# A graph-transformer layer on one core: the query row of the edge loop goes through PSUM, copied there by ScalarE

## The reference, cut to what matters

```python
def _L0_gnn_ref(feats, edge_index, edge_attr, Wq, bq, Wk, bk, Wv, bv, Wo, bo):
    q, k, v = ...                       # feats @ W.T + b, as 8 heads of 32
    r, c = edge_index[:, 0], edge_index[:, 1]
    sim = jnp.einsum('hed,hed->eh', q[:, c, :], k[:, r, :]) * scale
    m = jax.ops.segment_max(sim, c, num_segments=bs)
    p = jnp.exp(sim - m[c])
    attn = p / jax.ops.segment_sum(p, c, num_segments=bs)[c]
    agg = jax.ops.segment_sum((attn.T[..., None] * v[:, r, :]).transpose(1, 0, 2)..., c, ...)
    return agg @ Wo.T + bo

xn = _layernorm(x)
x = x + _L0_gnn_ref(xn, [src, dst], ...) + _L0_mix_ref(xn, w_qkv, w_out, b_out)   # linear attention
x = x + _L0_ffn_ref(_layernorm(x), ...)      # 8 experts, one per token, capacity limited
```

## Time and profile before

| | |
|---|---|
| time, median of 3 runs | 3486.49 us (3481.72 to 3488.05) |
| the profiled execution's own time | 3486.49 us |
| its span, first to last instruction | 3485.3 us |
| VectorE busy | 2388.3 us, 69% |
| GpSimd busy | 2430.6 us, 70% |
| TensorE busy | 2314.7 us, 66% |
| ScalarE busy | 1002.9 us, 29% |

### The profile page before, as it was taken

One profiled execution on the slowest core, in us unless ns is written; L12 is line 12 of the kernel. 1 busy time (PEld: TensorE's weight loads), 2 busy tenths in 40 slices (PEclk: granted clock), 3 DMA queues, 4 the chain that ended last, 5 costly groups with the idle time before them and its releaser, 6 DMA issues. The chain is left out here.

```text
span 3485.3 us, 39176 instructions
## 1 busy us (share of the span) xinstructions
PE 2314.7 (66%) x9498; PEld 1804.6 (52%) x9499; DVE 2388.3 (69%) x3245; ACT 1002.9 (29%) x4232; POOL 2430.6 (70%) x2220
## 2 busy tenths in 40 slices
PE   2839337675676666676688768556555562659998
PEld 1527226554555555454466545444444442559998
DVE  2324249786776787698888867877888884636665
ACT  1513116454455455451011100000000000435543
POOL 5050578777777777787777777777777776447776
PEclk7858668887888788787888877776777876569999
DMA  4624466666666666667777777666666662823341
GB/s 132 207 71 146 123 174 177 187 189 189 185 178 183 187 184 180 188 190 200 217 219 218 221 210 214 189 179 179 182 188 181 185 182 99 286 75 86 81 95 25
DMA packets 258264, 590.77 MB, mean 170 GB/s; under 512 B 49410, under 2 KB 135505, under 8 KB 257565
## 3 DMA queue, kind: packets, MB, share of 16 engines
q0 software_dynamic: 150480, 467.10, 49.3%
q1 hardware_dynamic: 97947, 109.47, 9.5%
q10 hardware_dynamic: 9296, 9.44, 0.8%
HBM read 519.05 MB, written 71.76 MB: 170 GB/s over the span
## 5 line engine op out<-in xcount | busy, mean ns | idle before, releaser
L959 POOL DMA_INDIRECT wide<-kv_d,arena x1099 | 1262.7, 1149 | 368.8 <-issue 344.9
L1253 PE MATMUL ps<-wide,arena 128*128 128x264 f32 x2432 | 782.2, 482 | 373.8 <-issue 219.1
L1253 PEld LDWEIGHTS ps<-wide,arena 128*128 128x128 f32 x2432 | 573.1, 241 | 568.2 <-issue 275.0
L959 POOL DMA_INDIRECT arena<-kv_d,arena x539 | 623.6, 1157 | 182.8 <-issue 165.4
L1356 DVE TENSOR_REDUCE arena<-arena 128x64 f32<-128x2048 f32 x229 | 523.5, 2286 | 7.9
L1253 PE MATMUL ps<-arena 128*128 128x264 f32 x1216 | 385.4, 476 | 174.6 <-issue 103.6
L1353 DVE TENSOR_TENSOR arena<-wide 128x2048 f32<-128x2048 f32 x153 | 350.8, 2293 | 185.1 <-DMA wide<-kv_d,arena 173.8
L1253 PEld LDWEIGHTS ps<-arena 128*128 128x128 f32 x1216 | 283.0, 238 | 272.9 <-issue 135.1
L1389 DVE TENSOR_TENSOR wide<-wide,ps 128x2112 f32<-128x2112 f32 x152 | 356.8, 2347 | 77.8 <-issue 39.0
L134 PE MATMUL ps<-halves 128*128 128x256 f32 (+2 forms) x2304 | 361.3, 319 | 3.2 <-DVE halves L1622 1.6
L134 PEld LDWEIGHTS ps<-halves 128*128 128x128 f32 x2304 | 331.0, 192 | 30.9 <-POOL halves L1632 3.5
(11 more groups left out here) (319 smaller groups left out, 3343.1 us busy)
## 6 DMA issues: line engine op xcount, KB each, us to landing
wide<-kv_d,arena POOLq DMA_INDIRECT x1099
arena<-in_w SPq DMA_DIRECT2D x16, 1024.0 KB
kv_d<-wide SPq DMA_DIRECT2D x49, 260.0 KB
arena<-xn_d SPq DMA_DIRECT2D x98, 128.0 KB
arena<-kv_d,arena POOLq DMA_INDIRECT x539
hb_d<-arena SPq DMA_DIRECT2D x16, 516.0 KB, 4.4
q_d<-wide SPq DMA_DIRECT2D x49, 128.0 KB
xn_d<-arena SPq DMA_DIRECT2D x7, 896.0 KB, 8.0
```

Source lines behind the costliest of these rows:

```text
L959: e.indirect_dma_start(out=kvb[k][:, j, :], out_offset=None, in_=kv_d, in_offset=bass.IndirectOffsetOnAxis(ap=ixb[k][:, j:j + 1], axis=0)) ...
L1253: m = e.matmul(psE[(k + 1) % 3][:, 0:264], ident, kvb[b][:, j, 256:ROW], start=(j == 0), stop=(j == J - 1))
```

## The change

ScalarE copies the query row of the next step from SBUF into a PSUM bank that the loop did not use (`ps[2]`), right behind `e_prod` and ahead of its copy of the indices. VectorE's L1353 reads the row from there and waits for the new semaphore `e_q` as well. The offset of the row is now loaded by ScalarE and no longer by VectorE.

```diff
-        p_ps, S_ps = ps[3][:, 0:8 * J], S_sb
+        q_ps, p_ps, S_ps = ps[2][:, 0:256], ps[3][:, 0:8 * J], S_sb
...
         def _(e):                                   # scalar
             e.wait_ge(e_n0, 1)
+            e.activation(q_ps, qsf[:, 0:256], ACT.Copy).then_inc(e_q, 1)
...
-                e.load([w_], tabF[:, bass.ds(at * 4 + 2, 1)])
+                e.load([w_, q_at], tabF[:, bass.ds(at * 4 + 2, 2)])
                 e.load([t6, w6, p6], tabF[:, bass.ds(at * 4 + 4 * RING - 1, 3)])
                 e.wait_ge(e_prod, g_)
+                e.activation(q_ps, qsf[:, bass.ds(val(e, q_at, NT * BLK) * 5, 256)], ACT.Copy).then_inc(e_q, 1)
                 e.activation(ixb[k], ixf[...], ACT.Copy).then_inc(e_ix, 1)
...
-            def scores(k, count, arrived, q_row):
+            def scores(k, count, arrived):
+                e.wait_ge(e_q, count)
                 e.wait_ge(e_arr[k], arrived)
                 e.tensor_tensor(prod.rearrange("p (j n) -> p j n", n=256), kvb[k][:, :, 0:256],
-                                q_row.unsqueeze(1).to_broadcast([128, J, 256]), ALU.mult).then_inc(e_prod, 1)
+                                q_ps.unsqueeze(1).to_broadcast([128, J, 256]), ALU.mult).then_inc(e_prod, 1)
...
-                e.load([ar, p, w_, q_at], tabF[:, bass.ds(val(e, cg, CH - 14) * 4, 4)])
+                e.load([ar, p, w_], tabF[:, bass.ds(val(e, cg, CH - 14) * 4, 3)])
...
-                scores((k + 1) % RING, cn, ar, qsf[:, bass.ds(val(e, q_at, NT * BLK) * 5, 256)])
+                scores((k + 1) % RING, cn, ar)
```

## The result

The changed kernel took 3511.61 us (median of four runs, 3503.78 to 3516.84) where the kernel before took 3484.10 beside it (3478.4 to 3488.05): a ratio of 1.0079, with an interval of 1.0056 to 1.0101. Forecast were 3367 us. The sign is wrong, and the mechanism at the centre of the forecast, gathers held by the product's second SBUF operand, is right.

What follows compares the result with a forecast made beforehand. GpSimd was taken to bound the edge loop, with VectorE 214 us behind. The span's 3485.3 − 214.0 + 70 + 25 = 3366.3, plus 1.2 around it, gave 3367 us; range for 8 in 10: 3285 to 3432.

Steps and rivals of the forecast that it cites:

- The gathers are held by a second SBUF operand: GpSimd's gathers beside VectorE's L1353, which reads two SBUF tensors, are held up; 325 us in all.
- GpSimd at 2120 us: GpSimd's edge loop once gathers are free: 2438 − 325 + about 7 for small operations.
- without a pause: GpSimd was said to work through the whole edge loop: 1886.3 us busy plus 551.6 idle ahead of gathers.
- The hidden copy: ScalarE's query copy and address, 0.48 us a step, 109 us in all, fit its idle time; no cost in ordinary steps.
- the bound of −10: VectorE's product reading PSUM: its own time changes by 0, between −10 and +20 ns each, ±5 us.
- VectorE's other waits stay: VectorE's waits other than for gathers remain, such as L1389's 155.8 us for ScalarE and short ones at L1370.
- floor of 2243: VectorE's loop of about 2457 us needs about 2243 without its 214.0 us of gather waits, and sets the end.
- The new wait, 14 × 5.0 = 70 us: VectorE's product waits for a late ScalarE copy, 5.0 us more in each of 14 steps; bounds 0 and 85.
- 25 us not won: Gather waits of VectorE ahead of long ScalarE waits, 14 × 1.8 us, give no gain; bounds 0 and 40.
- A: Rival: VectorE's new wait costs nothing because ScalarE's lateness moves with VectorE; 3273 us, chance 0.12.
- B: Rival: where base tiles move beside gathers, DMA transfers take 64 us of the gain; 3431 us, chance 0.13.
- C: Rival: gathers are still held beside the product, GpSimd stays the bound, the new wait is paid; 3541 us, chance 0.06.

Runs made afterwards that it cites:

- first comparison: The changed kernel against the kernel before, on a chip that is not known: 3511.61 us against 3484.10, ratio 1.0079.
- half the sums: TensorE adds only every second edge's values; in the changed kernel 3060.41 us (0.9123) on chip 4, 3497.50 us (1.0033) on chip 3.
- GpSimd paused: The "one copy" kernel with six chained small memsets on GpSimd ahead of every step's gathers, on chip 4: 3658.92 us, 1.0907 of the kernel before.
- the wait alone: The changed kernel with copy and wait, but the product reads SBUF as before; against the kernel before 1.0063 on chip 9, 0.9979 on chip 14.
- one copy again: The "one copy" kernel repeated on chip 14, against the kernel before: 3063.01 us, 0.9123.
- one copy: The changed kernel with the query row copied to PSUM once ahead of the loop and no per-step wait, on chip 9: 3531.15 us, 1.0053 of before.

## Why the prediction was wrong

The chips seen are of two kinds, and what the change does hangs on the kind (profiled executions; idle time is VectorE's, in the loop):

| | before, us | change, ratio | before: loop, idle | change: loop, idle | held-up matmuls, full sums |
|---|---|---|---|---|---|
| chips 2, 4, 14 | 3354 to 3357 | 0.9126 | 2397, 464 | 2120, 204 | none |
| first comparison, chips 3, 9 | 3484 to 3511 | 1.0079, 1.0073 | 2461, 528 | 2522, 599 | 175 to 333 us |

The loops are those of chip 2 (before) and chip 14 (change), and of the first comparison. The unaltered change ran on one chip of the first kind; on chip 4 it ran with half the sums and came out the same. On the second kind it ran in the first comparison and on chip 3, not on chip 9. No chip is known to have been measured at two different times, so "kind of chip" can also mean what else the machine was doing then. On the second kind VectorE's idle time stays between 516 and 614 us in all nine profiles: with the wait or without, with freed gathers or held ones, with half the sums. On the first kind it follows the gathers: 452 to 464 us with held ones, 202 to 204 with free ones, 766 with GpSimd paused. I take the cause of the difference to be in the machine, not in the program: the same program shows it on some chips and not on others. What it is stays open. That instructions reach the engines late is one candidate, since single ones come in steps of 0.7 and 1.4 us. The queue that loads them moves as much (502 packets, 4.11 MB, 0.4% of the DMA engines' time) in either, which does not tell how late they come; TensorE's mean granted clock is 0.80 after in the first comparison and 0.84 on chip 14, which at that size explains no spacing of 2.8 us. No run tried another placement of instructions.

By the prediction's own steps:

**The gathers are held by a second SBUF operand: right,** on both kinds. Gathers of the change on chip 14, and of before on chip 2 (min/median/max ns):

```profile
L959 POOL DMA_INDIRECT wide<-kv_d,arena x1099: 947/953/1214, 386.5 to 2470.3; - x184
```
```profile
L959 POOL DMA_INDIRECT wide<-kv_d,arena x1099: 949/953/3066, 389.8 to 2763.1; - x184
```

By the Trainium skill's page "SBUF — State Buffer", section "Who interferes with whom", a VectorE instruction with two inputs in SBUF contends with a GpSimd instruction that reads SBUF; the traces agree, and "the wait alone", with its 1162 ns, bears it out again. The same section's inference that a tensor_tensor does not hold back the making of DMA descriptors does not hold for these gathers: up to 3.07 us beside one, at most 1.21 with the operand in PSUM.

**GpSimd at 2120 us: near, and by luck closer than it looks.** VectorE's loop on chip 14 is 2120.1 us. But what the prediction summed, the gathers and the idle time ahead of them, is 2085 us there, and its starting value of 2438 held hold-ups: the idle part is 551.6 us in the first comparison and 499.2 on chip 2, so "without a pause" was wrong by some 50 us. Page groups on chip 14:

```profile
L959 POOL DMA_INDIRECT wide<-kv_d,arena x1099 | 1054.1, 959 | 344.2 <-issue 332.5
L959 POOL DMA_INDIRECT arena<-kv_d,arena x539 | 517.8, 961 | 169.1 <-issue 163.7
...
L1106 ACT ACTIVATE ps<-arena 128x64 f32<-128x64 f32 x228 | 51.9, 228 | 1004.0 <-DVE arena L1410 995.9
...
L1356 DVE TENSOR_TENSOR arena<-wide,ps 128x2048 f32<-128x2048 f32 x153 | 349.0, 2281 | 48.2 <-DMA wide<-kv_d,arena 48.1
L1392 DVE TENSOR_TENSOR wide<-wide,ps 128x2112 f32<-128x2112 f32 x152 | 356.6, 2346 | 0.0
...
L1373 DVE TENSOR_TENSOR arena<-arena,ps 128x264 f32<-128x264 f32 x230 | 96.7, 420 | 95.0 <-issue 94.8
```

GpSimd is busy 1571.9 us and idle 513.3, of which 496.1 are the gap between two gathers. VectorE is close behind: of its 2120 us it is busy in some 1917 and idle in 204, of which 95 are at the turn, 27 at the ends of tiles and 55 for gathers. The hidden copy holds too ("one copy again" is within 0.2 us). The product's time fell by 11 ns, 2.5 us in all, a little beyond the bound of −10; the 65 ns of the prediction's estimate for a PSUM source do not appear. Both kinds agree in this.

**"VectorE's other waits stay": the step that failed.** The sum took away the 214 us of waits for gathers and kept VectorE's floor of 2243, with 70 + 25 us for the new wait. In the first comparison the waits for gathers went as forecast, to 10 us, but the rest of VectorE's idle time, 528 − 214 = 314 us, did not stay: it became 599 − 10 = 589. That is 275 us more where 95 were in the sum. With 28 us that came back behind the loop it made the profiled execution 36 us longer, where 119 less were forecast.

The premise behind it was that these waits belong to the program. I took L1389's 155.8 us for ScalarE's own lateness. On the first kind of chip they are 0.5 us in the kernel before, and VectorE waits 330 us for gathers in place of 214:

```profile
L1389 DVE TENSOR_TENSOR wide<-wide,ps 128x2112 f32<-128x2112 f32 x152 | 356.7, 2347 | 0.5 <-ACT arena L1105 0.5
L1353 DVE TENSOR_TENSOR arena<-wide 128x2048 f32<-128x2048 f32 x153 | 351.4, 2297 | 272.1 <-DMA wide<-kv_d,arena 271.3
```

The floor there is 2397 − 330 = 2067 us and not 2243, GpSimd's 2085 stand above it, and the change wins 291 us, 172 more than forecast (119); 277 of them are in the loop. The forecast is as wrong on this kind as on the other, only with the right sign.

**The new wait, 14 × 5.0 = 70 us, and 25 us not won.** That the idle time not for gathers is 595 us (614 − 19) in "one copy" as well shows that the wait is not what makes it grow. On chip 14 the product waits for ScalarE's copy 5.7 us in all. Why hold-ups fill whatever the gathers give back on the second kind is not explained by any run; it is only measured. On chip 9 the held-up spacing is 212 us with held gathers ("the wait alone") and 272 to 333 in the three kernels with free ones, so it grows with the pace of the gathers but is not made by it alone. The 25 us had a slip of their own: 1.8 us is the mean of those waits that are not zero, and over all 14 steps it is 1.4, so 20 us.

**The rivals.** A's mechanism, that the new wait costs nothing, holds on chip 14, but its time of 3273 is 0.939 of the kernel before and not 0.9126, since it keeps the same floor. B (transfers take part of the gain) is refuted there: where base tiles move (1300 to 1600 us) the DMA engines are busy 0.82 of the time at 244 GB/s, and in the whole loop VectorE waits 55 us for gathers in place of 330. C gave the right sign on the second kind for a wrong reason: no gather is held. None of the rivals had the machine itself in it, though the trace spoke of it. In the list of waits of the kernel before, from the first comparison:

```profile
ACT ps L1104 <- issue: 575.9, 136, 9.2
...
POOL wide L959 <- issue: 344.9, 1079, 8.4
```

and on chip 2:

```profile
ACT ps L1104 <- DVE arena L1407: 1205.9, 227, 9.4
...
POOL wide L959 <- issue: 333.4, 1094, 0.3
```

(Engine, tile, line, what was waited for: us in all, times, longest.) ScalarE, which on chip 2 waits for VectorE 227 times of 228, waited 576 us for nothing that the profile shows, and GpSimd's gap of 0.3 us once lasted 8.4. I put the first down as spare time of ScalarE and did not read the longest of the second. Those rows were a reason for a range that holds both answers.

No version beats the change on chips 2, 4 and 14 (3060 with half the sums is the same within 0.1%), and on the others none that keeps all the sums beats the kernel before.

## What to carry to other kernels

A VectorE product from SBUF and SBUF beside indirect gathers is worth a PSUM operand: it gave GpSimd 0.18 to 0.21 us per gather on every chip where kernels with and without it were traced, but time only where nothing else held VectorE. Before building a floor from waits of the second engine, look whether they have a releaser at all: long waits for "issue" or "remote" on an engine whose work was ready, and single gaps of 8 us where the usual one is 0.3, need not belong to the program; here they were gone on three chips and took the gain on the others. The name alone does not tell: the 80 to 100 us of "issue" at the turn stayed on every chip. What tells is the start-to-start time of instructions that wait for no semaphore. Run such a change on more than one chip, always beside the kernel before.

## What the runs showed of the hardware

- One program, one chip type, two times: the kernel before takes 3354 to 3357 us on three chips and 3484 to 3511 on three measurements elsewhere. The slower ones lose some 50 us ahead of the loop too (it starts at 453.8 us in the first comparison and at 402.4 on chip 2).
- There TensorE's ready matmuls come 1.4, 2.1 or 2.8 us apart at times, and its single instructions, weight loads counted, 0.7 or 1.4; ready activations 1.4. In the eight profiles from chips 2, 4 and 14 there is none of it.
- A VectorE product of 2048 fp32 elements costs 2282 ns with one operand in PSUM and 2293 ns from SBUF alone.
- A memset on GpSimd of 32 elements is busy 0.13 us, but one that waits for the one before it costs 0.34 us (462.3 us for 1368).
